# A graph attention layer in one pass: row windows kept in SBUF instead of a spill between stages, and one of two one-hot builds moved to ScalarE

## Chip, cores and metric

The kernel runs on one core of a Trainium2 chip. The metric is the device time of one execution in microseconds. The program is one launch; all work on the indices (sorting by source, positions, tile boundaries) is done on the chip.

## What is computed

The inputs are 3125 nodes with 256 features, and 50000 edges sorted by destination. The reference, cut to what matters:

```python
x = layernorm(x + relu(concat([x, segment_sum(w * x[dst], src)]) @ W + b))   # first layer
# then two graph attention layers, on the edges and one loop per node:
xl = (x @ Wl).reshape(n, 8, 32);  xr = (x @ Wr).reshape(n, 8, 32)
e = leaky_relu(xl[src] + xr[dst], 0.2)
score = einsum('ehc,hc->eh', e, att)
smax = segment_max(score, dst)
ex = exp(score - smax[dst]);  denom = segment_sum(ex, dst)
out = segment_sum(ex / denom[dst] * xl[src], dst) + b
x = x + gelu(out)
# at the end: x = layernorm(x1 + x), x1 being the result of the first layer
```

## The kernel before

The 50000 edges lie in blocks of 128 ("slots"): slot i has one edge on each of the 128 partitions, and all its edges have their destination in one tile of 128 nodes. A slot of edges at a tile boundary is present once for each of the tiles. There are 416 slots (`NI`), 104 groups of four (`G`, `NG`), 25 node tiles (`NT`) and 8 heads (`H`). All arithmetic is fp32.

The program is a row of stages with a barrier of all engines behind each. Within a stage every engine has its own loop over groups, and semaphores order them.

- Preparation (0 to 170 us): positions, tile tables, columns per slot, and `RST`, the reset table of the maxima.
- Scatter (170 to 826): for each group SyncE broadcasts the four slots' local destinations into `LBC` (two buffers, line 446), VectorE makes the transposed one-hot `OHT` of them (L458) and copies indices (L461, L462), PE expands node rows by it (L474), ScalarE weights them (L489), and GpSimd writes them to DRAM at their place by source (indirect transfers, L502).
- Sums by source (826 to 1074), the dense first layer and layer norm (to 1157).
- Then for each of two attention layers: a linear stage (1157 to 1232 in the first; VectorE's L829 to L848, 25 tiles), which also writes the table of rows (`tab_d`, 264 wide: 256 features and 8 linear score parts) to DRAM and keeps `TARGET`, the 272 wide part of the destinations, in SBUF;
- scoring (1232 to 1889): VectorE's one-hot (L927), PE's expansion of the destination's part (L913), GpSimd's indirect gather of the source's rows (L877) from indices that ScalarE copies (L980), the sum of both on VectorE (L934), Relu on ScalarE (L973), the weighting (L939) and reduction to scores (L942). SyncE writes every gathered group back to DRAM (`spill_d`, 544 KB for each group, L885);
- maxima (1889 to 1980): barred scores of all slots are transposed to rows, two scans forward and backward give the maximum of each destination over its run of edges (L1031 to L1048), with a trip to DRAM between for the carries between 16 chunks; then the shift and Exp for all slots (L1053, L1096);
- sums (1980 to 2294): 128 visits (104 groups and 24 boundaries). SyncE loads a spilled group (L1152), ScalarE appends its exponentials (L1174), VectorE and GpSimd weight two of its slots each (L1142), VectorE makes the one-hot `OH` of the destinations (L1198, L1203), PE multiplies (L1188), and VectorE adds the result to the tile's sums `ACC` (L1211);
- the close (2294 to 2350): the loop's own share, the division by the denominator, bias, Gelu and addition.

The second attention layer takes 2350 to 3527, a last layer norm ends at 3562. In the scoring stage VectorE's order is written by hand: one-hot of group q, sum of expansion and row of group q-1, score of group q-2. GpSimd fetches four groups ahead at most, into the four buffers of `GATH`, each of which is free when its spill has landed and Relu of its group is through.

## Time and profile before

| | us |
|---|---|
| median of 3 runs | 3580.03 |
| lowest, highest | 3555.76, 3587.68 |
| the profiled execution | 3563.68 |
| its span, first to last instruction | 3561.9 |
| mean granted TensorE clock, share of 2.4 GHz | 0.789 |
| PE busy | 1870.6 (53%) |
| VectorE (DVE) busy | 2152.1 (60%) |
| GpSimd (POOL) busy | 1762.4 (49%) |
| ScalarE (ACT) busy | 687.7 (19%) |
| moved by DMA | 559.52 MB |

In the rows further below, a line such as L934 is the kernel's line; "out<-in" are the program's names; x is a count; "idle before" is how long the engine had nothing to do before the instruction, and the arrow names what ended it, as far as the profile could tell. Indirect transfers on GpSimd show their issue, not their landing. Times of PE are modelled at their ends.

### The profile page before, as it was taken

What the parts mean: (1) busy time and instruction counts of PE and PEld (TensorE: products, weight loads), DVE (VectorE), ACT (ScalarE), POOL (GpSimd) and SP (SyncE); (2) the same over time, 40 slices, a digit from 0 to 9 for tenths busy, and PEclk for the clock granted to TensorE, in tenths of its full rate; (3) what the DMA queues carried; (4) which work ended last, traced back from release to release, by engine and by line L of the source; (5) the groups of instructions that cost most, each with busy time, mean ns of one, the idle gap of its engine ahead of it and who ended that gap; (6) DMA issues with size and microseconds to landing.
All of it is one profiled execution on the core that took longest, in us unless ns stands there. A gap on an engine that the chain in (4) does not pass through costs nothing. (4 is left out here: it accounts for less than half of the span.)

```text
span 3561.9 us, 40332 instructions
## 1 busy us (share of the span) xinstructions
PE 1870.6 (53%) x6284; PEld 1298.6 (36%) x6285; DVE 2152.1 (60%) x3331; ACT 687.7 (19%) x1987; POOL 1762.4 (49%) x1670
## 2 busy tenths in 40 slices
PE   0144444446996744544441688654454454248880
PEld 0133333335775323323321455422333333135560
DVE  6511111114664756666667799985666675779997
ACT  0022222220001322222221211132222221121111
POOL 0266666661002266666662455535666666325555
PEclk9976666668998866777675899977768777679995
DMA  1133333337991266666661577615666676237763
GB/s 54 23 108 101 101 100 103 100 101 205 266 261 40 76 193 189 206 190 206 187 205 37 183 225 231 200 36 164 193 199 213 195 214 200 68 124 228 231 218 110
DMA packets 271165, 559.52 MB, mean 157 GB/s; under 512 B 40988, under 2 KB 172352, under 8 KB 271134
## 3 DMA queue, kind: packets, MB, share of 16 engines
q1 hardware_dynamic: 210590, 394.18, 35.2%
q0 software_dynamic: 60544, 165.02, 16.4%
q14 instruction: 23, 0.19, 0.0%
q8 instruction: 8, 0.13, 0.0%
HBM read 377.24 MB, written 185.14 MB: 158 GB/s over the span
## 5 line engine op out<-in xcount | busy, mean ns | idle before, releaser
L877 POOL DMA_INDIRECT gath<-gather_table,GIDX x832 | 841.4, 1011 | 474.0 <-issue 257.6
L913 PE MATMUL p_expd<-node,OHT 128*128 x1664 | 615.5, 532 | 687.8 <-DVE OHT L927 487.3
L913 PEld LDWEIGHTS p_expd<-node,OHT 128*128 128x128 f32 x1664 | 406.0, 256 | 898.0 <-issue 803.3
L1188 PE MATMUL p_sums<-gath,OH 128*128 128x272 f32 x2048 | 536.9, 407 | 125.5 <-DVE OH L1203 101.2
L502 POOL DMA_INDIRECT rows_by_src<-gath,GIDX x416 | 411.7, 990 | 257.3 <-ACT gath L489 137.3
L1142 POOL TENSOR_TENSOR gath<-gath 128x512 f32<-128x512 f32 x256 | 323.7, 1266 | 435.1 <-ACT gath L1174 434.7
L934 DVE TENSOR_TENSOR work<-p_expd,gath 128x1056 f32<-128x1056 f32 x208 | 260.9, 1254 | 436.8 <-DMA chunk_carry<-by_head 182.4
L1188 PEld LDWEIGHTS p_sums<-gath,OH 128*128 128x128 f32 x2048 | 372.6, 191 | 289.4 <-issue 146.5
L474 PE MATMUL p_expd<-X,OHT 128*128 x832 | 285.8, 511 | 348.5 <-ACT gath L489 186.3
L474 PEld LDWEIGHTS p_expd<-X,OHT 128*128 128x128 f32 x832 | 208.8, 260 | 425.1 <-issue 385.5
L942 DVE TENSOR_REDUCE arena<-work 128x1056 f32 (+1 forms) x208 | 260.6, 1253 | 29.8
L939 DVE TENSOR_TENSOR work<-work,VEC 128x1024 f32<-128x1024 f32 x208 | 253.9, 1221 | 0.0
L489 ACT ACTIVATE gath<-p_expd,WGT 128x256 f32<-128x256 f32 x416 | 161.4, 481 | 467.9 <-remote 359.5
L580 PE MATMUL p_sums<-gath,OH 128*128 128x256 f32 x976 | 228.8, 388 | 42.5 <-DVE OH L553 41.8
L1203 DVE TENSOR_TENSOR OH<-iota_row,dst_local 128x512 f32<-128x512 f32 x256 | 250.9, 980 | 0.0
L458 DVE TENSOR_SCALAR OHT<-LBC,iota_p 128x512 f32<-128x512 bf16 x104 | 51.5, 496 | 325.2 <-remote 217.7
L971 ACT ACTIVATE arena<-p_expd 128x32 f32 (+1 forms) x208 | 41.2, 198 | 1008.2 <-DVE work L934 604.1
L973 ACT ACTIVATE work<-work 128x1024 f32<-128x1024 f32 x208 | 218.3, 1049 | 0.0
L580 PEld LDWEIGHTS p_sums<-gath,OH 128*128 128x128 f32 x976 | 181.6, 191 | 89.9 <-DVE OH L553 33.4
L1142 DVE TENSOR_TENSOR gath<-gath 128x512 f32<-128x512 f32 x256 | 193.7, 757 | 14.4 <-ACT gath L1174 13.1
L461 DVE CAST gath<-SRCI 128x4 f32 (+1 forms) x104 | 20.9, 201 | 226.8 <-DMA rows_by_src<-gath,GIDX 170.3
L1198 DVE TENSOR_TENSOR dst_local<-dst_visit,FIRST 128x4 f32<-128x4 f32 x256 | 121.6, 475 | 25.3 <-ACT dst_visit L1172 16.0
(189 smaller groups left out, 1781.5 us busy)
## 6 DMA issues: line engine op xcount, KB each, us to landing
gath<-gathered SPq DMA_DIRECT2D x256, 544.0 KB
gathered<-gath SPq DMA_DIRECT2D x208, 544.0 KB
gath<-rows_by_src SPq DMA_DIRECT2D x122, 514.0 KB
LBC<-local_rows SPq DMA_DIRECT2D x312, 128.0 KB
gath<-gather_table,GIDX POOLq DMA_INDIRECT x832
rows_by_src<-gath,GIDX POOLq DMA_INDIRECT x416
gather_table<-arena SPq DMA_DIRECT2D x50, 132.0 KB, 1.7
arena<-gather_table SPq DMA_DIRECT2D x10, 640.0 KB
```

Source lines behind the costliest of these rows:

```text
L474: ins = pe.matmul(expd[s % 2][:, g // 2, (g % 2) * D:(g % 2 + 1) * D], OHT[:, s % 2, g * P:(g + 1) * P], Xv[:, bass.ds(j, 1), :], start=Tr ...
L502: pool.indirect_dma_start(sup_d[:, :], bass.IndirectOffsetOnAxis(GIDX[:, s, g:g + 1], 0), U[:, s, g, :], None, bounds_check=EP - 1, oob_is ...
L580: ins = pe.matmul(sums[s][:, 0:D], OH[:, s % 2, g, :], U[:, s, g, 0:D], start=(g == 0), stop=(g == G - 1))
L877: pool.indirect_dma_start(GATH[:, s, g, 0:XW], None, tab_d[:, :], bass.IndirectOffsetOnAxis(GIDX[:, s, g:g + 1], 0)).then_inc(gathered[s], 16)
L913: ins = pe.matmul(expd[s % 2][:, g, 0:RW], OHT[:, s % 2, g * P:(g + 1) * P], TARGET[:, bass.ds(j, 1), :], start=True, stop=True)
L934: dve.tensor_tensor(Zv[:, s4 % 2], expd[s4 % 2][:, :, 0:XW], GATH[:, s4, :, 0:XW], ALU.add).then_inc(z_ready, 1)
L939: dve.tensor_tensor(TR, TR, VEC[:, 2, :].rearrange("p (h c) -> p h c", h=H).unsqueeze(1).broadcast_to([P, G, H, C]), ALU.mult).then_inc(we ...
L942: dve.tensor_reduce(SC[:, bass.ds(G * H * q, G * H)], T[:, s2, :].rearrange("p (g c) -> p g c", c=C + 1), AX, ALU.add).then_inc(scored, 1)
L973: act.activation(Tv[:, s % 2, :, :, 0:C], Zv[:, s % 2, :, 0:D].rearrange("p g (h c) -> p g h c", h=H), ACT.Relu).then_inc(relu_ready, 1)
L1142: return eng.tensor_tensor(V, V, GATH[:, s, g0:g1, D:D + H].unsqueeze(3).broadcast_to([P, g1 - g0, H, C]), ALU.mult)
L1188: ins = pe.matmul(sums[s][:, 0:RW], OH[:, s % 2, g, :], GATH[:, s, g, :], start=(g == 0), stop=(g == G - 1))
L1203: dve.tensor_tensor(OH[:, s % 2], iota_row[:, :].unsqueeze(1).broadcast_to([P, G, P]), LS[:, s % 2, :].unsqueeze(2).broadcast_to([P, G, P] ...
```

## The change

The three stages scoring, maxima and sums of an attention layer become one, in which everything is unrolled.

- Slots come in pairs of one tile, so 440 rather than 416 slots, and 110 groups of four. Four groups are a window of 16 slots, of which there are 28. One slot's 8 heads by 16 slots are 128 columns.
- Gathered rows stay in `ROWS`, a ring of 12 groups in SBUF; there is no spill. The indices are read from `SRCI` itself. GpSimd gathers group q behind its share of the weighting of group q-10.
- A group's score is made as before. When a window's scores are there, VectorE bars them (`bar`), PE transposes them, and VectorE scans forward and backward over 128 columns (`ends`), works out the carries between slots on one partition (`carry`), scans again with them (`maximum`), and shifts (`shift`); ScalarE makes the exponentials and a factor `GROW`, by which the sums of a tile that reaches over a window's boundary are scaled (`grow`). The carries go through PE, not DRAM.
- Sums are taken eight steps (`LAG`) behind the expansion, two tiles per group and so two additions into `ACC` (`add_sums`).
- The one-hot of the sums is made by ScalarE: |column - destination| for each slot (`own`), then Relu(1 - that) for four (`own_end`). The transposed one-hot of the expansion stays on VectorE (`hot`).
- The score of a node's own loop is no longer expanded per slot but kept per node (`OWN`), and joins at the close, where the edges' sums are scaled by Exp of the difference of maxima. The linear stage forms less for it.
- `LBC` has four buffers, also in the scatter stage, which is unrolled too and loses the copy at L462.
- Preparation fetches one more column (next destination), and the tables of resets are per window.

```diff
+PAIRS = (NB + 2 * NT - 1) // 2
+NI = -(-2 * PAIRS // G) * G
+K = P // H
+WG = K // G
+NW = -(-NI // K)
+RING = 3 * WG
+LAG = 2 * WG
...
-                                dve.tensor_tensor(LIN, LR[:, s, :, 0:D], VEC[:, 1, :].unsqueeze(1).broadcast_to([P, 2, D]),
-                                                  ALU.mult).then_inc(lin_ready, 1)
+                                dve.tensor_tensor(LIN, LR[:, s, 0, 0:D], VEC[:, 1, :], ALU.mult).then_inc(lin_ready, 1)
...
+                    @block.sync
+                    def _(sp):
+                        for q in range(NG):
+                            if q >= 4:
+                                sp.wait_ge(hot_t, q - 3)
+                            sp.dma_start(LBC[:, q % 4, :], locals_of(q)).then_inc(loc_in[q % 4], 16)
 
                     @block.gpsimd
                     def _(pool):
+                        def gather(q):
+                            if q >= RING:
+                                pool.wait_ge(summed, q - RING + 1)
+                            pool.nop(nofuse=True)
+                            for g in range(G):
+                                i = G * q + g
+                                pool.indirect_dma_start(ROWS[:, i % (RING * G), 0:XW], None, tab_d[:, :],
+                                                        bass.IndirectOffsetOnAxis(SRCI[:, i:i + 1], 0)).then_inc(gathered[q % RING], 16)
+
+                        for q in range(NG + RING - 2):
+                            a = q - RING + 2
+                            if a >= 0:
+                                pool.wait_ge(exps, a // WG + 1)
+                                weigh(pool, a, 0, 2).then_inc(by_pool, 1)
+                            if q < NG:
+                                gather(q)
...
+                        expand(0)
+                        for t in range(STEPS):
+                            if t + 1 < NG:
+                                expand(t + 1)
+                            u = t // WG - 1
+                            if 0 <= u < NW and t % WG == 0:
...
+                                pe.wait_ge(barred, u + 1)
+                                pe.transpose(BY_ROW, BARRED[:, :, :].rearrange("p h k -> p (h k)"), ident[:, :]).then_inc(by_row, 1)
...
+                            a = t - LAG
+                            if 0 <= a < NG:
+                                pe.wait_ge(hots, a + 1)
+                                pe.wait_ge(by_pool, a + 1)
+                                pe.wait_ge(by_dve, a + 1)
+                                pe.wait_ge(added, 2 * a)
+                                for g in range(G):
+                                    ins = pe.matmul(sums[g // 2][:, 0:RW], OH[:, a % 2, g, :], slots(a, g, g + 1)[:, 0, :], start=(g % 2 == 0), stop=(g % 2 == 1))
+                                ins.then_inc(summed, 1)
...
+                        def ends(u):
+                            dve.wait_ge(by_row, u + 1)
+                            if u:
+                                dve.wait_ge(final, u)
+                            dve.tensor_scalar(HOT[:, :], iota_row[0:1, :], NLOC[0:1, K * u:K * u + 1], 0.0, ALU.add, ALU.is_equal)
+                            link(dve.tensor_tensor_scan(FWD[:, :], RST[:, u, 0:P], BY_ROW, -BIG, ALU.add, ALU.max))
+                            dve.tensor_tensor_scan(BWD[:, ::-1], RST[:, u, 1:P + 1][:, ::-1], FWD[:, ::-1], -BIG, ALU.add, ALU.max).then_inc(ends_ready, 1)
...
+                        def add_sums(a, tiles):
+                            dve.wait_ge(summed, a + 1)
+                            for k in range(2):
+                                j = tiles[2 * (a % WG) + k]
+                                dve.tensor_tensor(ACC[:, bass.ds(j, 1), :], ACC[:, bass.ds(j, 1), :], sums[k][:, 0:RW].unsqueeze(1), ALU.add).then_inc(added, 1)
+                                dve.wait_ge(added, 2 * a + k + 1)
...
+                        for t in range(STEPS):
+                            if due(t, 2):
+                                shift(t // WG - 2)
+                            if t < NG:
+                                add(t)
+                            if t + 2 < NG:
+                                hot(t + 2)
+                            u = t // WG - 1
+                            if 0 <= u < NW and t % WG:
+                                (ends, carry, maximum)[t % WG - 1](u)
+                            if 0 < t <= NG:
+                                score(t - 1)
+                            if due(t, 1):
+                                bar(u)
+                            a = t - LAG
+                            if 1 <= a <= NG:
+                                add_sums(a - 1, tiles)
+                            if a >= 0 and a % WG == 0 and a < NG:
+                                tiles = tiles_of(dve, 2 * a, 2 * groups(a // WG))
+                                if a:
+                                    grow(a // WG, tiles[0])
+                            if 0 <= a < NG:
+                                dve.wait_ge(exps, a // WG + 1)
+                                weigh(dve, a, 2, G).then_inc(by_dve, 1)
...
+                        def own(a):
+                            if a >= 2:
+                                act.wait_ge(summed, a - 1)
+                            for g in range(G):
+                                i = G * a + g
+                                ins = act.activation(OH[:, a % 2, g, :], iota_row[:, :], ACT.Abs, bias=NLOC[:, i:i + 1])
+                            ins.then_inc(near, 1)
+
+                        def own_end(a, n):
+                            act.wait_ge(near, n)
+                            act.activation(OH[:, a % 2], OH[:, a % 2], ACT.Relu, bias=ones[:, 0:1], scale=-1.0).then_inc(hots, 1)
```

## Rows read from the trace of the kernel before

**Rows 1.** Windows by stage: stretch, length, busy us of PE, PEld, DVE, ACT, POOL (instructions), clock, DMA share, GB/s

```profile
170.00:826.00 656.00, 285.78 (x832) 208.83 (x832) 75.98 (x312) 162.68 (x417) 414.71 (x417) 0.69 0.33 99
...
1157.00:1232.00 75.00, 56.49 (x150) 24.54 (x150) 61.69 (x177) 30.11 (x75) 11.65 (x25) 0.91 0.19 64
1232.00:1889.00 657.00, 303.70 (x832) 199.59 (x832) 415.20 (x416) 141.99 (x417) 427.01 (x416) 0.72 0.64 195
1889.00:1980.00 91.00, 11.16 (x52) 10.12 (x52) 57.47 (x24) 14.95 (x18) 17.66 (x3) 0.52 0.03 6
1980.00:2294.00 314.00, 267.82 (x1024) 186.24 (x1024) 302.64 (x510) 58.97 (x255) 160.73 (x128) 0.99 0.72 225
```

**Rows 2.** Timeline of DVE in the scoring stage: start us, us, engine, line, operation

```profile
1504.08 0.48 DVE L927 TENSOR_SCALAR OHT<-LBC,iota_p 128x512 f32<-128x512 bf16 x1
1504.47 1.25 DVE L934 TENSOR_TENSOR work<-p_expd,gath 128x1056 f32<-128x1056 f32 x1
1505.64 1.22 DVE L939 TENSOR_TENSOR work<-work,VEC 128x1024 f32<-128x1024 f32 x1
1507.01 1.25 DVE L942 TENSOR_REDUCE arena<-work 128x1056 f32 x1
1508.18 0.48 DVE L927 TENSOR_SCALAR OHT<-LBC,iota_p 128x512 f32<-128x512 bf16 x1
```

**Rows 3.** Groups of instructions: count, busy us and mean ns of one, idle before, releaser

```profile
L1142 POOL TENSOR_TENSOR gath<-gath 128x512 f32<-128x512 f32 x256 | 323.7, 1266 | 435.1 <-ACT gath L1174 434.7
...
L973 ACT ACTIVATE work<-work 128x1024 f32<-128x1024 f32 x208 | 218.3, 1049 | 0.0
...
L1211 DVE TENSOR_TENSOR node<-node,p_sums 128x272 f32 x256 | 108.8, 425 | 3.0 <-PE p_sums L1188 2.2 <-DVE node L1211 0.8
...
L975 ACT ACTIVATE work<-work 128x32 f32<-128x32 f32 x208 | 51.7, 248 | 0.0
...
L1092 ACT ACTIVATE arena<-p_f 128x512 f32<-128x512 f32 (+1 forms) x28 | 15.1, 568 | 137.3 <-PE p_f L1082 114.5 <-PE p_f L1073 22.7
...
L1096 ACT ACT_TABLE_LOAD x2 | 2.6, 1283 | 0.0
```

**Rows 4.** Timelines of DVE and POOL in the sums stage

```profile
2127.64 0.69 DVE L1142 TENSOR_TENSOR gath<-gath 128x512 f32<-128x512 f32 x1
2128.25 1.54 DVE L1203 TENSOR_TENSOR OH<-iota_row,dst_local 128x512 f32<-128x512 f32 x1
...
2127.69 1.55 POOL L1142 TENSOR_TENSOR gath<-gath 128x512 f32<-128x512 f32 x1 [1.80 <-ACT gath L1174]
```

**Rows 5.** Groups of instructions: small operations and scans of DVE

```profile
L1047 DVE TENSOR_TENSOR_SCAN gath<-arena,carries 128x3328 f32<-128x3328 f32 x2 | 14.3, 7151 | 22.9 <-DMA carries<-chunk_carry 22.9
...
L840 DVE TENSOR_TENSOR arena<-arena 128x8 f32<-128x8 f32 x50 | 7.9, 157 | 0.0
...
L1040 DVE TENSOR_TENSOR_SCAN by_head<-by_head 8x16 f32<-8x16 f32 x2 | 0.4, 178 | 9.6 <-DMA by_head<-chunk_summary 9.6
```

**Rows 6.** A stall in scoring (POOL, DVE); its waits, 1240 to 1880: us, times, longest

```profile
1514.31 0.96 POOL L877 DMA_INDIRECT gath<-gather_table,GIDX  x1 [0.30 <-issue]
...
1515.59 1.26 DVE L934 TENSOR_TENSOR work<-p_expd,gath 128x1056 f32<-128x1056 f32 x1 [6.94 <-DMA FIRST<-step_tables]
...
DVE work L934 <- DMA FIRST<-step_tables: 166.3, 23, 11.4
```

**Rows 7.** Timelines of POOL and ACT in the scatter stage

```profile
454.89 0.98 POOL L502 DMA_INDIRECT rows_by_src<-gath,GIDX  x1 [0.30 <-issue]
461.33 0.98 POOL L502 DMA_INDIRECT rows_by_src<-gath,GIDX  x1 [5.46 <-ACT gath L489]
...
458.92 1.21 ACT L489 ACTIVATE gath<-p_expd,WGT 128x256 f32<-128x256 f32 x3 [11.06 <-remote]
```

**Rows 8.** Timeline of PE: one group's expansion, then one group's sums

```profile
1509.53 3.18 PE L913 MATMUL p_expd<-node,OHT 128*128 x8 [2.24 <-issue]
...
2289.53 2.10 PE L1188 MATMUL p_sums<-gath,OH 128*128 128x272 f32 x8
```

More of the change, by code:

```diff
@@ L861, in build @@
[L861 to L867 removed]
+                expd = [ps(f"expd{k}", [P, 2, 512]) for k in range(2)]
+                sums = [ps(f"sums{k}", [P, 512]) for k in range(2)]
+                cols = ps("cols", [P, 512])
+                rows = ps("rows", [P, 512])
+                BY_ROW, FINAL = cols[:, 0:P], cols[:, P:2 * P]
@@ L929, in add, with hot @@
-                        def add(q, s4, turn4, first):
-                            dve.wait_ge(gathered[s4], 64 * (turn4 + 1))
-                            dve.wait_ge(exp_ready, q + 1)
-                            if not first:
+                        dve.memset(SC[:, :, :], 0.0)
+                        dve.memset(BARRED[:, :, :], -BIG)
+                        link(dve.memset(line[:, :], -BIG))
+                        dve.memset(CR[:, :], 0.0).then_inc(set_up, 1)
+                        def hot(q):
+                            dve.wait_ge(loc_in[q % 4], 16 * (q // 4 + 1))
+                            if q >= 2:
+                                dve.wait_ge(expanded, q - 1)
+                            dve.tensor_scalar(OHT[:, q % 2, :], LBC[:, q % 4, :], iota_p[:, 0:1], None, ALU.is_equal).then_inc(hot_t, 1)
```

874 lines of the change are left out of this document (387 added, 487 removed).

## Prediction

> **What bounds the kernel now.** I read first the windows by stage [rows 1], to see which engine is full in each stage that the change touches. The first graph layer's middle is three stages: the expansion and scoring (657 us), the maxima (91) and the sums (314), 1062 us in all; I take the second layer for the same. In the sums VectorE is full (302.6 of 314). In the scoring nobody is: VectorE works 415 of 657 us, GpSimd 427, and the DMA engines move 195 GB/s, to which the spill of the gathered rows belongs. In the maxima all engines together do little.
>
> Then VectorE's timeline in a stretch of the scoring without stalls [rows 2]: from one start of L927 to the next are 4.10 us for a group of four slots. That is less than its four instructions one by one (4.20), since the end of one overlaps the start of the next; behind L939, where the next waits for a semaphore of its own engine, it does not (1.37 us from start to start for 1.22 of work, 0.15 for the link). A group needs four row transfers of GpSimd, each 0.96 us behind a gap of 0.30, 5.06 us [rows 6]. So GpSimd's transfers, 104 x 5.06 = 526 us, are the floor of the scoring, and some 130 us are stalls. What they look like is in [rows 6]: the sum at L934 starts at 1515.59 after 6.94 us of idleness, when GpSimd has just finished its last queued transfer (1514.31 + 0.96). Such waits are 166 us in 23 pieces in this stage. The scatter stage ahead (170 to 826) has the same shape with no spill at all: 104 groups in 656 us, 6.3 us each, though GpSimd issues them in 5.15 (0.98 and a gap of 0.30 each); again and again it falls quiet, as for 5.46 us behind the transfer at 454.89 [rows 7].
>
> **The change, part by part.** (1) *The new single pass.* 110 groups of four slots in windows of four groups; a group is summed eight steps after it is expanded. VectorE's work for a step in the middle: the expansion's sum, now 1024 wide (1.14 from start to start), the one-hot (0.39), weighting with its link (1.37) and the reduction (1.17): 4.07 us [rows 2]. Then two additions into the node sums for one before, 128x272 at 0.42 [rows 3], each with a link of 0.15: 1.14. Then half of the weighting of the rows, 0.60 from start to start [rows 4]. The one-hot for the sums, 0.68 here, has gone to ScalarE. Together 5.81 us.
>
> Once per window come the maxima. Small operations cost 0.16 (8 wide) [rows 5] to 0.42 (272 wide) [rows 3], so 0.28 at 128; a scan has a fixed 0.14 and 2.1 ns a column (178 ns for 16 columns, 7.15 us for 3328), so 0.42 for 128 [rows 5]. Barring and shifting: three of 128, 0.8. `ends`: one small, two scans and a link, 1.1. `carry`: two scans, three copies or sums of 128, four of 8 and five links, 3.1, less four overlaps of 0.08, 2.8. `maximum`: one small, two scans, two links, 1.3. `grow`: one of 256, one of 8, a link, 0.7. The register loads, a guess by the link's size, 0.4. Sum 7.1, or 1.78 a step. So 7.6 us a step before anyone disturbs anyone.
>
> Of contention the sums stage has the nearest row, since there too GpSimd weights two slots per group beside VectorE: a weighting of 1.55 us on GpSimd stands over a VectorE instruction of 1.54 that elsewhere takes 0.68 [rows 4]. Over the stage VectorE is busy 302.6/128 = 2.36 us a visit, where its four instructions undisturbed need 0.68 + 0.68 + 0.42 + 0.16 = 1.94 [rows 1, 3, 4, 5]: 0.42 lost per GpSimd weighting. Bounds are 0 and 0.86 (every one collides in full); I take 0.42, for the same pair of operations is in the row. A step is 8.0 us. [...]
>
> (2) *Who else could set the step.* GpSimd: 5.06 for the transfers plus 1.27 for the weighting [rows 3] and gaps, 6.6 us: under 8.0, with some 5 us over per window. PE: eight passes for the expansion and eight for the sums take 2.1 us each at full clock (the second of [rows 8]), and eleven small ones per window, by the same 0.26 a pass, 0.75 a step: 5 us. ScalarE: Relu 1.05 and its tail 0.25, the one-hot as four of 128 columns (0.3 each, between nothing and the 0.57 for 512) and one of 512 (0.57): 3.1, with the window's six small ones 3.5 [rows 3]. All three lie under VectorE's step, and their results are asked for a step later: the sums of group a-1 begin when its weighting ends, need 2.1 us, and VectorE comes to add them 4 us into the next step. So the one-hot on ScalarE costs nothing, as long as VectorE's 8.0 us cover it. Exp, Relu, Abs and Copy alternate in a window. One table load takes 1.28 us and stands once per layer for Exp [rows 3]; four loads per window would be 1.3 us a step on ScalarE, still covered. By "ScalarE: Activation LUTs", section "Table sets: the hidden batching unit", in the Trainium skill all of these lie in one set and none is needed; the trace agrees, with no load at the Relu that follows another layer's Gelu.
>
> (3) *The pass as a whole.* The first eight steps have no sums and go at GpSimd's pace: 8 x 5.1 and 3 of landing, with one stall like that of [rows 6] 52 us. 102 full steps: 816. The tail of eight, in which weighting, PE's 2.1, addition and little else follow each other, 3.6 us each: 29. The stage's start, 3. Sum 900, against 1062: -162 a layer, -324 for two. No spill is written or read back; as no stage waits for DMA bandwidth in the new order, that is in the figure already.
>
> (4) *The scatter stage.* 110 groups rather than 104, four buffers for the local rows rather than two, one copy less. At its old 6.3 us a group, 693: +37. If the buffers take the stalls away, 110 x 5.15 + 10 = 577: -79. But in such a spell ScalarE too starts only at 458.92, 3 us after GpSimd's last transfer, though it does not wait for those buffers [rows 7]; so I keep +37.
>
> (5) *Smaller ones.* Preparation: four more transfers (5), two reductions of 3584 columns (8), some ten small chained operations (3), strided loads (4): +20. The linear stage (75 us, VectorE 61.7 of it): per tile one multiplication and one reduction 256 wide rather than 512, and a small sum less, 0.7 us, 17 in 25 tiles; PE is busy 56 us there, so I take -12 a layer. The memset of the sums goes to its end on GpSimd, which has been done by then. The closing stage: six more operations of 200 columns and two Exps with a wait, +3 a layer; the large multiplication by the denominators is only replaced. The first dense stage loses a memset: -1.
>
> Sum: -324 + 37 + 20 - 24 + 6 - 1 = -286. From the span of 3562: 3276; the run is 2 longer than its span, and the median of the runs 16 above the profiled one: 3294, said as 3295.
>
> **The rivals.** *R1, the stalls come along (slower).* VectorE is full in the new pass, so a late arrival ahead of its sum of expansion and row is lost time. The place is the wait of `add` for rows and expansion. For it: these waits stand in both stages with GpSimd transfers [rows 6, 7], and in the new pass each transfer group leads its use by only two steps at the start of a window. Against: GpSimd is at it 5.06 of 8.0 us (63%), not 5.15 of 6.3 (82%), with a weighting in between and a spell of quiet per window, and the spill is gone. Price as now, 166 us x 110/104 = 176 a layer: 3295 + 352 = 3647. It decides from 142 us a layer on, 1.3 us a step. *R2, every GpSimd weighting collides in full*: 0.44 x 204 = +90: 3385. *R3, PE's clock stays at 1.2 GHz, the lower of its two levels.* Then eight passes take up to twice 2.1 us (3.18 in the first of [rows 8], where the clock was low for a part), the step 4.2 + 4.2 + 1.5 = 9.9, and PE is the bound: +388, 3683. Against it: with PE at work 5 of 8 us, more than in the scoring stage (46% and clock 0.72), it should hold. *R4, better all round*: no collisions (-86) and the scatter stage without stalls (-116): 3093. That the change does not do what it says is no case here: the stages are gone from the program.
>
> **How the numbers follow.** The forecast 0.5 (own range 3230 to 3350), R1 0.18, R2 0.15, R3 0.05, R4 0.12. The range, 3110 to 3580, leaves out most of R1 and R3 and the end of R4. About 1% is what a measurement of this kernel can tell from no change (its three runs span 0.9%). Faster: forecast, R2 and R4, 0.77, and 0.01 of R1, whose price may be half. Within 1%: 0.05, from R1 and R3 near the threshold. Slower: the rest of them, 0.17.
>
> **What would show it.** In the profile after: one stage per layer of some 890 us with VectorE over 90% busy; start to start of the sum of expansion and row 7.5 to 8.4 us in the middle; the added idleness ahead of that sum under 50 us a layer (R1: over 150); GpSimd's weighting near 1.3 us and VectorE's own at 0.7 to 0.9 (R2: over 1.3); the clock over 0.9 in the pass (R3: under 0.7); the scatter stage near 690 us. I am wrong if a serial exchange between VectorE and PE inside a window, which I let overlap, shows as idleness of VectorE, or if the 25 small operations per window cost far more than 7.1 us.

## The result, and the profile after

The changed kernel takes 3318.7 us in the median (3312 to 3327) beside 3580.8 for the kernel before: a ratio of 0.928 (95% interval 0.923 to 0.933). Forecast were 3295 us and a range of 3110 to 3580; the time lies 24 us above the forecast.

For what follows one thing has to be known: the kernel before itself runs at two levels, 3332 to 3338 us in some sittings (runs made together on one chip) and 3546 to 3581 in others, so only runs of one sitting, or stages that do not depend on it, are compared below.

Table 1: the length of each stage, from the first VectorE instruction of one to that of the next, in the two profiled executions (before 3561.9 us, after 3316.4 us).

| stage | before | after | difference | forecast |
|---|---|---|---|---|
| preparation | 171.2 | 192.1 | +21 | +20 |
| scatter | 656.4 | 669.7 | +13 | +37 |
| sums by source | 254.8 | 255.2 | 0 | 0 |
| first dense stage | 83.0 | 82.1 | -1 | -1 |
| linear, both layers | 71.2 + 71.4 | 55.4 + 56.1 | -31 | -24 |
| middle of layer 1 | 1058.8 | 928.7 | -130 | -162 |
| middle of layer 2 | 1049.4 | 929.2 | -120 | -162 |
| close, both layers, and end | 145.8 | 148.0 | +2 | +6 |
| sum | | | -245.5 | -286 |

The forecast's sum was 41 us too good. It came out only 24 us too low, since 16 us, the distance of the median from the profiled run of before, were added and did not come again. Of the 74 us that the two middles gained less than forecast, 58 are the new passes (929 us each instead of 900) and 16 the base: I had put the old middles at 1062 us each, and they measured 1059 and 1049.

First the windows of the profile after: the scatter stage, the new pass of layer 1, and a stretch of its middle; then the same pass in three parts. The columns are those of [rows 1].

```profile
192.00:862.00 670.00, 306.83 (x880) 221.69 (x880) 68.37 (x221) 172.06 (x441) 434.99 (x441) 0.68 0.35 99
1254.00:2183.00 929.00, 601.54 (x2124) 449.90 (x2124) 813.32 (x1332) 354.56 (x939) 589.96 (x550) 0.79 0.32 80
1350.00:2050.00 700.00, 467.18 (x1696) 354.05 (x1695) 651.66 (x1057) 280.67 (x748) 472.05 (x442) 0.81 0.33 85
...
1254.00:1324.00 70.00, 32.23 (x91) 22.33 (x92) 37.41 (x55) 12.18 (x24) 41.40 (x41) 0.65 0.38 104
1324.00:2124.00 800.00, 532.81 (x1935) 403.07 (x1933) 745.17 (x1205) 322.86 (x861) 542.45 (x504) 0.81 0.34 84
2124.00:2183.00 59.00, 36.51 (x100) 24.49 (x100) 30.74 (x74) 19.52 (x55) 6.11 (x6) 0.68 0.00 1
```

In the middle VectorE is busy 651.66 of 700 us, 93%: it is what sets the step, as forecast. The start, 70 us with VectorE half idle, and the end, 59 us, are not full. The granted clock is 0.81 in the middle, not over 0.9.

These are VectorE's groups in the same middle, 1350 to 2050 us (columns as in [rows 3]):

```profile
L1033 DVE TENSOR_TENSOR work<-p_expd,gath 128x1024 f32<-128x1024 f32 x88 | 107.1, 1217 | 3.3 <-PE p_expd L971 3.2
L1099 DVE TENSOR_TENSOR node<-node,p_sums 128x272 f32 x176 | 76.1, 432 | 12.6
L1106 DVE TENSOR_TENSOR node<-node,grow 128x256 f32 x22 | 32.3, 1469 | 17.4 <-issue 14.2 <-DVE node L1099 3.2
L1073 DVE TENSOR_TENSOR line<-line 1x8 f32<-1x8 f32 x22 | 24.6, 1120 | 0.8
L1071 DVE COPY line<-line 1x8 f32<-1x8 f32 x22 | 9.8, 447 | 0.8
```

Ahead of L1033, the sum of expansion and row, VectorE waits 3.3 us in 88 steps. That is the place of rival R1, and next to nothing is lost there. But an instruction of 8 columns takes 1.12 us in the mean (its neighbour of the same size 0.15), and the rescaling of a node tile, L1106, takes 1.47. What they wait for is seen when VectorE's and GpSimd's timelines of one window are laid side by side. VectorE:

```profile
1900.26 1.90 DVE L1106 TENSOR_TENSOR node<-node,grow 128x256 f32 x1 [0.79 <-DVE node L1099]
...
1907.82 1.01 DVE L1099 TENSOR_TENSOR node<-node,p_sums 128x272 f32 x2
...
1912.68 0.15 DVE L1072 TENSOR_TENSOR line<-line 1x8 f32<-1x8 f32 x1
1912.86 1.65 DVE L1073 TENSOR_TENSOR line<-line 1x8 f32<-1x8 f32 x1
1914.54 0.15 DVE L1074 TENSOR_TENSOR line<-line 1x8 f32<-1x8 f32 x1
1914.63 1.21 DVE L1039 TENSOR_TENSOR work<-work,VEC 128x1024 f32<-128x1024 f32 x1
```

and GpSimd:

```profile
1900.81 1.06 POOL L933 TENSOR_TENSOR gath<-gath 128x512 f32<-128x512 f32 x1
...
1907.45 1.06 POOL L933 TENSOR_TENSOR gath<-gath 128x512 f32<-128x512 f32 x1
...
1912.46 0.94 POOL L952 DMA_INDIRECT gath<-gather_table,SRCI  x1 [0.30 <-issue]
1913.41 1.06 POOL L933 TENSOR_TENSOR gath<-gath 128x512 f32<-128x512 f32 x1
1914.63 2.07 POOL L952 DMA_INDIRECT gath<-gather_table,SRCI  x1 [0.16 <-issue]
```

The 8-column sum at 1912.86 ends at 1914.51, when GpSimd's weighting has ended (1913.41 + 1.06 = 1914.47); L1106 ends at 1902.16, just behind the weighting that ends at 1901.87. Both start some 0.55 us before the recorded start of the weighting whose end they share (1912.86 against 1913.41, 1900.26 against 1900.81); why so early, these rows do not say. The additions at 1907.82, with an input in PSUM, keep their 1.01 us for two although a weighting runs beside them. And it goes the other way too: the transfer that GpSimd issues at 1914.63, the moment VectorE's L1039 begins, takes 2.07 us instead of 0.94.

### The profile page after: what moved, and what is told of

Same layout as the page of the kernel before. It is cut to its first block and busy times, and to the rows that moved or that the text cites. A ratio compares the mean times of both kernels' runs of the same rounds, so it can differ in the third digit from the quotient of the medians.

```text
span 3316.4 us, 30379 instructions
## 1 busy us (share of the span) xinstructions
PE 1910.8 (58%) x6768; PEld 1410.9 (43%) x6768; DVE 2217.8 (67%) x3985; ACT 980.3 (30%) x2514; POOL 1774.5 (54%) x1707
## 5 line engine op out<-in xcount | busy, mean ns | idle before, releaser
L952 POOL DMA_INDIRECT gath<-gather_table,SRCI x880 | 945.1, 1074 | 261.6 <-issue 232.4
L1009 PE MATMUL p_sums<-gath,OH 128*128 128x272 f32 x1760 | 658.4, 536 | 486.2 <-DVE gath L933 480.1
L525 POOL DMA_INDIRECT rows_by_src<-gath,node x440 | 430.1, 977 | 270.6 <-ACT gath L514 140.7
L971 PE MATMUL p_expd<-node,OHT 128*128 x1760 | 481.4, 423 | 39.4 <-DVE OHT L1026 24.4
L933 POOL TENSOR_TENSOR gath<-gath 128x512 f32<-128x512 f32 x220 | 234.0, 1066 | 407.2 <-ACT gath L1172 404.6
L514 ACT ACTIVATE gath<-p_expd,node 128x256 f32<-128x256 f32 x440 | 170.8, 479 | 478.9 <-remote 358.3
L1033 DVE TENSOR_TENSOR work<-p_expd,gath 128x1024 f32<-128x1024 f32 x220 | 267.8, 1217 | 50.1 <-remote 23.5
L1153 ACT ACTIVATE OH<-iota_row,NLOC 128x128 f32<-128x128 f32 x880 | 278.7, 387 | 60.4 <-PE p_sums L1009 56.1
L1043 DVE TENSOR_REDUCE scores<-work 128x32 f32<-128x1056 f32 x220 | 275.7, 1253 | 7.6
L1039 DVE TENSOR_TENSOR work<-work,VEC 128x1024 f32<-128x1024 f32 x220 | 265.6, 1207 | 0.0
L1099 DVE TENSOR_TENSOR node<-node,p_sums 128x272 f32 x440 | 190.3, 432 | 79.4 <-PE p_sums L1009 47.2
L933 DVE TENSOR_TENSOR gath<-gath 128x512 f32<-128x512 f32 x220 | 153.7, 699 | 8.1 <-issue 0.6
```

Source lines behind the costliest of these rows:

```text
L525: pool.indirect_dma_start(sup_d[:, :], bass.IndirectOffsetOnAxis(POSI[:, i:i + 1], 0), U[:, q % 4, g, :], None, bounds_check=EP - 1, oob_i ...
L933: return eng.tensor_tensor(R, R, V[:, :, D:XW].unsqueeze(3).broadcast_to([P, g1 - g0, H, C]), ALU.mult)
L952: pool.indirect_dma_start(ROWS[:, i % (RING * G), 0:XW], None, tab_d[:, :], bass.IndirectOffsetOnAxis(SRCI[:, i:i + 1], 0)).then_inc(gathe ...
L971: ins = pe.matmul(expd[q % 2][:, g // 2, (g % 2) * D:(g % 2 + 1) * D], OHT[:, q % 2, g * P:(g + 1) * P], TARGET[:, bass.ds(tiles[g // 2], ...
L1009: ins = pe.matmul(sums[g // 2][:, 0:RW], OH[:, a % 2, g, :], slots(a, g, g + 1)[:, 0, :], start=(g % 2 == 0), stop=(g % 2 == 1))
L1033: dve.tensor_tensor(Zv[:, q % 2].rearrange("p k (g n) -> p k g n", g=2), expd[q % 2][:, :, :].rearrange("p k (g n) -> p k g n", g=2), slot ...
```

## The experiments

All kernels are the changed one with the edit shown, unless said otherwise. Where a step is given, it is the time between the starts of the sum of expansion and row (L1033, in some variants L1029, L1027 or L1023), taken over 88 steps in the middle of layer 1's pass. This figure is the same in every sitting: 7.96, 7.96 and 7.95 us for the three kernels in which the middle of the pass is the changed kernel's (`after`, `ctl_after`, `early`).

**First sitting: the kernel before 3331.7 us.** Four kernels, the first on the pass, the others on the stalls of the scatter stage.

*h_dve*, the one-hot for the sums back on VectorE:

```diff
+ dve.scalar_tensor_tensor(OH[:, a % 2], iota_row..., -1.0, NLOC[:, G*a:G*a+G]..., ALU.mult, ALU.is_equal).then_inc(hots, 1)
  weigh(dve, a, 2, G).then_inc(by_dve, 1)
...
- own(a)
- own_end(a, a + 1)
```

> The changed kernel with the one-hot for the sums made by VectorE again (one instruction of 128x512 just ahead of its weighting), ScalarE's five instructions for it taken out. Theory (VectorE's own work sets the step of the single pass): each of the 102 full steps grows by the 0.68 us that this instruction took in the kernel before, so the pass by some 70 us a layer and the kernel from 3319 to about 3460; with collisions (it reads two inputs in SBUF beside GpSimd's weighting) up to 3530. Rival (the step is set by the exchange of VectorE with ScalarE and PE, or by GpSimd's transfers): VectorE has slack, and the time moves by less than 30 us.

Measured: 3301.2 us, 0.990 of the kernel before (0.988 to 0.993). The changed kernel itself takes 3194.4 in the next sitting, which is of the same kind, and its three variants below take 3192 to 3196 in this one. So the one-hot on ScalarE is worth 107 us of the 143 that the change brings in such a sitting; the rest of the change takes off 1% there. The step goes from 7.96 to 8.45: 0.49 us, less than 0.68. From the one-hot's start to the next instruction's are 0.61 us; 0.05 comes back because VectorE now loses 0.65 us a step to GpSimd's weighting and not 0.70 (the sum is shown under *w_dve*), and some 0.04 because the wait ahead of L1033 is gone. The theory holds, VectorE has next to no slack.

*s_pace*, a paced queue in the scatter stage:

```diff
  pool.wait_ge(u_ready, q + 1)
+ if q >= 3:
+     pool.wait_ge(scattered[(q - 3) % 4], 64 * ((q - 3) // 4 + 1))
```

> The changed kernel with one more wait in the scatter stage: GpSimd issues the transfers of a group only when those of the group three before have landed, so that the transfers under way at once are fewer. Theory P (the stalls of this stage come from a backlog of transfers, behind which everything else that travels by DMA queues up): with fewer under way the stalls go, the stage falls from 670 us to between 580 and 620, the kernel to 3230 to 3270. Rival (the backlog only sits in the queue and has nothing to do with the stalls): the stage stays at 670 or grows by the wait, to 700, the kernel at 3320 to 3350.

*s_tick*, a small computing instruction between the groups:

```diff
  pool.wait_ge(u_ready, q + 1)
+ pool.memset(TICK[:, q:q + 1], 0.0)
```

> The changed kernel with one small computing instruction of GpSimd (a memset of one column) ahead of each group of the scatter stage. Theory G (the stalls arise while GpSimd issues transfers back to back with nothing in between, which the single pass with its weighting never does once it runs full): the stalls of 8 to 12 us every seven groups go, the stage falls from 670 us to about 110 x 5.3 + 10 = 590, the kernel to 3240. Rival (the stalls are of the transfers, whatever GpSimd does in between): the stage stays at 660 to 680 us and the kernel at 3315 to 3330.

*s_two*, two local-row buffers in the scatter stage, as before:

```diff
- if q >= 4: sp.wait_ge(hot_ready, q - 3)
- sp.dma_start(LBC[:, q % 4, :], locals_of(q)).then_inc(loc_in[q % 4], 16)
+ if q >= 2: sp.wait_ge(hot_ready, q - 1)
+ sp.dma_start(LBC[:, q % 2, :], locals_of(q)).then_inc(loc_in[q % 2], 16)
```

> The changed kernel with two instead of four buffers for the local rows in the scatter stage, as before: that part of the change undone. In the prediction this edit was taken at nothing. Theory: the stalls do not hang on these buffers, the stage stays at 660 to 690 us and the kernel at 3310 to 3345. Rival (the buffers have taken some of the stalls away, and so the stage came out at 670 and not at the 693 forecast): the stage at 693 or more, the kernel at 3342 or more.

Measured: 3196.1, 3194.2 and 3192.3 us. Three different edits, one result, and a kernel before 250 us faster than the one first read: read against the 3319 us, each edit would have looked like the cure. None of them is. *h_dve* leaves the scatter stage as it is, and there too the stage takes 581 us in this sitting, as in the other three (581, 581 and 581). All three expectations had been written against the wrong base. Whether one of the edits would help where the stalls are, no run shows.

**Second sitting: the kernel before 3337.8 us.**

*ctl_after* is the changed kernel unaltered.

> The changed kernel itself, unaltered, as the control. Three variants of its scatter stage (a paced queue, a small instruction in between, two local-row buffers) all came out at 3192 to 3196 us beside a kernel before of 3332, though the times first shown for the two were 3319 and 3581. Theory S (the stalls with GpSimd's transfers are a matter of the chip the kernel runs on, not of the three edits): on a chip where the kernel before takes some 3330 us this one takes 3190 to 3200, a ratio of 0.958; on one where it takes some 3580 it takes 3310 to 3330, a ratio of 0.928. Rival (each of the three edits breaks the stalls): beside a kernel before of 3330 it takes 3300 or more.

Measured: 3194.4 us (3192 to 3195), ratio 0.958 (0.954 to 0.961). That is the figure of theory S, and the rival is out: the three edits of the first sitting are worth nothing there. That the level belongs to the chip is not shown. The first sitting and the third and fourth ran on a chip of the same number, 6, and the kernel before took 3332 us in the one and 3546 and 3551 in the others.

*ctl_before* is the kernel before, unaltered.

> The kernel before itself, unaltered, for its trace on this chip. Theory S: if its time here is some 3330 us, the 250 us less than in the trace first read lie in the stages with GpSimd's transfers: the scatter stage at 5.1 to 5.3 us a group, 540 to 560 us instead of 656, the two scoring stages at 550 to 590 us each instead of 657, and its waits of some 7 us that go as 'remote' gone. Rival (the whole chip is faster): the sums stages (314 us) and the source sums are shorter by 5% or more too.

Measured: 3333.9 us, span 3332.1. The windows of the scatter stage, layer 1's scoring and layer 1's sums in this sitting:

```profile
171.00:731.00 560.00, 305.35 (x832) 213.10 (x832) 82.08 (x312) 164.52 (x417) 415.69 (x417) 0.73 0.44 117
1139.00:1725.00 586.00, 337.93 (x832) 220.32 (x832) 419.88 (x416) 154.66 (x412) 450.67 (x415) 0.70 0.76 218
1812.00:2130.00 318.00, 268.50 (x1024) 186.56 (x1024) 304.54 (x511) 58.90 (x255) 159.30 (x128) 0.98 0.72 224
```

Against [rows 1]: scatter 560 instead of 656, scoring 586 instead of 655, the sums stage the same. VectorE's and GpSimd's busy times are no shorter (GpSimd's 416 and 451 us beside 415 and 427); only waits are gone. In this sitting the page also has a time from issue to landing for the scatter's transfers:

```profile
gath<-gather_table,GIDX POOLq DMA_INDIRECT x832, 3.7
rows_by_src<-gath,GIDX POOLq DMA_INDIRECT x416, 3.5
```

and the longest waits of the scatter stage are regular ones, many and short, with nothing that ends as "remote":

```profile
DVE gath L461 <- DMA rows_by_src<-gath,GIDX: 425.9, 100, 6.8
PEld p_expd L474 <- issue: 276.9, 95, 6.3
ACT gath L489 <- DVE GIDX L462: 276.3, 74, 5.5
```

The scatter stage of the changed kernel with stalls (3318 us) looks otherwise:

```profile
ACT gath L514 <- remote: 358.3, 41, 16.7
DVE OHT L488 <- remote: 209.1, 33, 12.1
```

So the stalls of [rows 6, 7] cost the kernel before 96 us in the scatter stage and 68 and 65 in the two scoring stages: 230 us, all of the difference between its two levels. In the changed kernel they cost 90 in the scatter stage and 12 and 18 in the two passes; over the whole span it is 124 us (3316.4 against 3192.8). What makes them come and go between sittings, no run here shows. They also set what the change is worth: by the profiled spans 245 us with the stalls and 139 without (by the medians 262 and 143).

*w_dve*, GpSimd weights nothing:

```diff
- weigh(pool, a, 0, 2).then_inc(by_pool, 1)
- pe.wait_ge(by_pool, a + 1)
- weigh(dve, a, 2, G).then_inc(by_dve, 1)
+ weigh(dve, a, 0, G).then_inc(by_dve, 1)
```

> The changed kernel with all four slots of a group weighted by VectorE and none by GpSimd. Theory C (GpSimd's weighting costs VectorE some 0.4 us per step by contention, as the prediction had it): VectorE's instruction goes from 0.70 to 1.2 us, the collisions go, a step grows by 0.1 to 0.3 us, the pass by 10 to 30 us a layer, the kernel by 20 to 60 us over the control. Rival N (no contention to speak of): plus 0.6 x 102 = 61 us a layer, 120 in all. Rival F (contention costs more than the half weighting saves): no more than the control, or less.

Measured: 3163.0 us (3162 to 3164), 31 us less than the control; step 7.72. It is rival F. Here are its groups in the middle:

```profile
L933 DVE TENSOR_TENSOR gath<-gath 128x1024 f32<-128x1024 f32 x85 | 104.3, 1227 | 3.0
L1022 DVE TENSOR_SCALAR OHT<-LBC,iota_p 128x512 f32<-128x512 bf16 x83 | 39.9, 481 | 0.0
L1102 DVE TENSOR_TENSOR node<-node,grow 128x256 f32 x21 | 8.9, 425 | 16.6 <-DVE node L1095 16.6
```

The rescaling is down from 1469 to 425 ns, with nothing changed about it but that GpSimd no longer computes. The other victims fall too. That gives the price of contention in the changed kernel, per window of four steps: (1469 - 425) ns for L1106, (1120 - 159) for L1073, (447 - 193) for L1071, four times (561 - 481) for the one-hot, 220 on two more of `carry`: 2.8 us, 0.70 us a step. The half weighting that GpSimd takes over is worth 1.15 - 0.61 = 0.54 from start to start. GpSimd's help costs more than it brings: 0.16 us a step by these rows, 0.24 by the step, of which 0.04 is the wait ahead of L1033 that is gone too.

*hg_act*, the one-hot for the expansion and the rescaling of a node tile go to ScalarE too:

```diff
+ act.activation(OHT[:, q % 2, :], LBC[:, q % 4, :], ACT.Abs, bias=minus_p[:, 0:1]).then_inc(far, 1)
+ act.activation(OHT[:, q % 2, :], OHT[:, q % 2, :], ACT.Relu, bias=ones[:, 0:1], scale=-1.0).then_inc(hot_t, 1)
+ for h in range(H):
+     R = ACC[:, bass.ds(tile, 1), h * C:(h + 1) * C]
+     ins = act.activation(R, R, ACT.Copy, scale=GROW[:, h:h + 1])
- dve.tensor_scalar(OHT[:, q % 2, :], LBC[:, q % 4, :], iota_p[:, 0:1], None, ALU.is_equal).then_inc(hot_t, 1)
- dve.tensor_tensor(R, R, GROW[:, :].unsqueeze(2).broadcast_to([P, H, C]), ALU.mult)
```

> The changed kernel with two more pieces of VectorE's work on ScalarE: the one-hot for the expansion too (Abs and Relu over 128x512), and the rescaling of a node tile at each window's start (eight instructions of 128x32 with a factor per partition). Theory (VectorE sets the step): VectorE loses 0.45 us a group and 1.4 us a window, so 110 x 0.45 + 27 x 1.4 = 87 us a layer, 170 in all: the ratio to the control about 0.947, start to start of the expansion's sum 7.1 instead of 7.9 us. GpSimd, with 5.0 + 1.1 us and gaps a step, is then near. Rival (with ScalarE at 5 us a step and more exchange, the chain through ScalarE and PE sets the step): less than 60 us of gain, or a loss, with VectorE idle at the sum of expansion and row or at the additions of the sums.

Measured: 3044.6 us (3043 to 3046), 0.913 of the kernel before (0.910 to 0.916) and 150 us less than the control; step 7.21. The theory, with a gain 20 us smaller than it gave; ScalarE's added work is hidden.

**Third sitting: the kernel before 3546.1 us.**

*h_act* has only the first of these two moves.

> The changed kernel with only the one-hot for the expansion moved to ScalarE too (the rescaling of the node tile stays on VectorE): the first half of the run with both moves, to split its gain of 150 us. Theory (VectorE's own work adds up to the step): start to start of this instruction is 0.39 to 0.48 us, 110 groups, two layers: 85 to 105 us less than the control's 3194, so 3090 to 3110, a step of 7.5 us, and the other 45 to 65 us of the double move belong to the rescaling. Rival (the instruction filled time in which VectorE would have waited for GpSimd's lock anyway): the wait moves to the next instruction with two inputs in SBUF, and the gain is under 60 us.

Measured: 3182.7 us, a ratio of 0.898 (0.896 to 0.901). The times in the expectation were for the other kind of sitting, so the step has to decide: 7.26 us. It gains 0.70, not 0.39 to 0.48, and the rescaling brings only 0.05 more. The groups of its middle say why:

```profile
L1033 DVE TENSOR_TENSOR work<-work,VEC 128x1024 f32<-128x1024 f32 x97 | 124.1, 1280 | 0.0
L933 DVE TENSOR_TENSOR gath<-gath 128x512 f32<-128x512 f32 x96 | 84.9, 885 | 3.3
L1060 DVE TENSOR_TENSOR_SCAN line<-line 1x136 f32<-1x136 f32 x24 | 16.0, 665 | 0.8
L1100 DVE TENSOR_TENSOR node<-node,grow 128x256 f32 x24 | 10.2, 425 | 19.3 <-DVE node L1093 18.2 <-issue 1.1
```

With one instruction fewer in the step GpSimd's weighting meets others. The rescaling is back at 425 ns and the 8-column sum at 0.16 us, while the weighting (885 for 690), the multiplication (1280 for 1205) and one scan (665 for 429) now take longer: 0.35 us a step instead of 0.70. So about half the gain is VectorE's instruction taken away, and the other half is contention that fell away with it. The theory was right in its kind, not in its split. The rival is out.

*hgw* has both moves, and VectorE weights all four slots.

> The kernel with both moves to ScalarE, and in addition all four slots weighted by VectorE, none by GpSimd. In the control the same edit gained 31 us. Theory (what GpSimd's weighting costs VectorE depends on which instructions it happens to meet, and can be summed from the excess of each row over its undisturbed time): with both moves that excess is 0.27 + 0.06 on the weighting and the multiplication and 0.3 us a window on a scan, 0.43 us a step in all instead of 0.8, so giving GpSimd's half back to VectorE (0.61) costs 0.18 a step: 3045 + 37 = 3080. Rival (the cost is a constant of each weighting): the gain of 31 us comes again, 3014.

Measured: 3203.3 us, a ratio of 0.904 (0.901 to 0.906). The expected 3080 and 3014 us were for a sitting without stalls, and hg_act did not run in this one, so again the step has to decide: 7.27, against 7.21 for hg_act. The same edit that gained 0.24 us a step in the changed kernel costs 0.06 here. That decides against the rival (a constant price per weighting); the sum from the rows, +0.18, has the sign right and is 0.12 too high; 0.07 of that is the half weighting, taken as 0.61 and worth 0.54.

*early* weights a group before the sums of the group ahead are added:

```diff
+ weigh(dve, a, 2, G).then_inc(by_dve, 1)
  add_sums(a - 1, tiles)
  ...
- weigh(dve, a, 2, G).then_inc(by_dve, 1)
```

> The changed kernel with VectorE weighting group a before, not behind, the addition of the sums of group a-1. Theory (the last eight groups of a pass go at 6 to 7 us each, not at the 3.6 of the prediction, because weighting, PE's sums at its lower clock, addition and the next weighting follow each other in a ring): PE's sums of a group can start right behind the additions, the ring loses the 0.7 us of the weighting, 8 groups, two layers: 10 to 15 us less, 3180 to 3185, and the middle of the pass stays at 7.96 us a step. Rival (in the middle the later additions hold up PE's next sums): the step grows and the kernel with it, 3200 or more.

Measured: 3271.5 us, a ratio of 0.923 (0.921 to 0.926). The changed kernel had 0.928 (0.923 to 0.933) in another sitting of this kind; the intervals overlap, and the times in the expectation were for a sitting without stalls. So the trace has to decide. This is PE in the last steps of the changed kernel's pass:

```profile
2164.56 3.06 PE L1009 MATMUL p_sums<-gath,OH 128*128 128x272 f32 x8 [2.04 <-DVE gath L933]
2170.80 3.97 PE L1009 MATMUL p_sums<-gath,OH 128*128 128x272 f32 x8 [3.18 <-DVE gath L933]
2176.80 3.97 PE L1009 MATMUL p_sums<-gath,OH 128*128 128x272 f32 x8 [2.03 <-DVE gath L933]
```

and VectorE beside it:

```profile
2169.86 0.69 DVE L933 TENSOR_TENSOR gath<-gath 128x512 f32<-128x512 f32 x1
2174.81 1.02 DVE L1099 TENSOR_TENSOR node<-node,p_sums 128x272 f32 x2 [4.26 <-PE p_sums L1009]
2175.86 0.69 DVE L933 TENSOR_TENSOR gath<-gath 128x512 f32<-128x512 f32 x1
2180.91 1.02 DVE L1099 TENSOR_TENSOR node<-node,p_sums 128x272 f32 x2 [4.37 <-PE p_sums L1009]
```

Each waits for the other in turn: weighting, PE's sums, addition, weighting, a ring of 6.0 us a group. In `early` the stretch from the last L1033 to the end of the pass is 45 us, in the changed kernel 59 and in the control 62, while the middle keeps its 7.95 us: the rival, a longer step, is out. The end gave back more than the 0.7 us a group expected, 1.8 to 2.1. Its two halves in `early` (columns as in [rows 1]), with PE's sums in them, show what the rest is:

```profile
2108.00:2130.00 22.00, 16.42 (x43) 10.53 (x41) 15.84 (x35) 9.35 (x27) 3.88 (x4) 0.52 0.00 0
2130.00:2153.00 23.00, 13.36 (x56) 9.27 (x55) 14.40 (x40) 9.91 (x29) 3.25 (x3) 1.00 0.00 1
...
2125.25 3.97 PE L1009 MATMUL p_sums<-gath,OH 128*128 128x272 f32 x8 [1.09 <-DVE node L1099]
...
2134.42 2.07 PE L1009 MATMUL p_sums<-gath,OH 128*128 128x272 f32 x8 [1.22 <-DVE node L1099]
2138.13 2.07 PE L1009 MATMUL p_sums<-gath,OH 128*128 128x272 f32 x8 [1.20 <-DVE node L1099]
```

From 2130 on the granted clock is 1.00, the eight passes take 2.07 us instead of 3.97, and the groups follow each other at 3.3 to 3.9 us. In the changed kernel the clock of the whole end is 0.68 and in the control 0.64, and at most one of their ten groups has 2.07 us. So the larger part of what `early` brought is PE's clock at the end of the pass, the smaller the order. Whether the order is what raised the clock, one profile does not show.

**Fourth sitting: the kernel before 3550.5 us.** *hge* puts hg_act and early together.

> All that has gained put together: both one-hots and the rescaling of the node tile on ScalarE, and VectorE's weighting ahead of the addition of the sums. Theory (the gains are independent: 0.75 us a step for the moves, some 17 us a pass at its end for the order): beside a kernel before of 3330 to 3340 it takes 3045 - 34 = 3010, a ratio of 0.90; beside one of 3550 to 3580 some 3140, a ratio of 0.885. Start to start 7.2 us in the middle, and 45 us or less from the last sum of expansion and row to the end of the pass, instead of 62. Rival (with the step at 7.2 us the later additions hold up PE's next sums, and VectorE waits for them): the ratio stays where the double move without the new order had it, 0.913 in the first case.

Measured: 3161.0 us (3156 to 3168), a ratio of 0.889 (0.887 to 0.892), the best of all in a sitting of this kind: 0.928 for the change alone, 0.898 for h_act. The theory had 0.885 and some 3140 us. The end of the pass is 48 us, but the step 7.29, not 7.21. VectorE does not wait longer for PE's sums, as the rival had it (13.2 us of idleness ahead of 179 additions in the middle, 12.6 ahead of 172 in hg_act). GpSimd's weighting has found another victim, the last 8 columns of the rescaling:

```profile
L1101 DVE TENSOR_TENSOR node<-node,grow 128x8 f32 x23 | 38.3, 1663 | 18.7 <-DVE node L1095 15.4 <-issue 3.3
```

It takes 0.17 us in hg_act and 1.66 here: 0.37 us a step more. Some 0.2 of that comes back at other instructions (the weighting 824 ns instead of 913, a scan 428 instead of 764), which leaves about the 0.08 by which the step is longer, and a little over.

## Why the prediction came out as it did

**The step of 8.0 us: right, by terms that were off and cancel.** It measured 7.96. VectorE's own instructions for a step take 5.62 us in the timeline instead of 5.81 (the additions 1.04 for two instead of 1.14, multiplication and reduction 2.41 instead of 2.54, the one-hot 0.42), the window's small ones about 1.64 a step instead of 1.78. In the 1.78 the part for `ends` was summed as 1.1 us a window, where its own terms give 1.27; with it the forecast of the step would have been 0.04 longer. Contention, taken as 0.42 from [rows 4], is 0.70. It was within the bounds of 0 and 0.86, but the row gave its size and not its victims. In the sums stage the victim was a large instruction; here VectorE's own weighting stays at 0.69, and what pays is whichever instruction the weighting happens to meet, down to one of 8 columns. The Trainium skill's page "SBUF — State Buffer", section "Who interferes with whom", says that the shared ports are an exclusive lock, in which the later one waits for the whole instruction of the other; the trace agrees (1914.51 against 1914.47). The size of the waiting instruction therefore says nothing of the price. That the step came out at 8.0 all the same is luck: contention 0.28 too low against the other terms 0.33 too high.

**ScalarE's one-hot at nothing: right.** h_dve undid it and lost 107 us, and it is the larger part of what the change is worth without stalls. Its four small instructions take 0.387 us and the large one 0.707, not 0.3 and 0.57, and still vanish under the step: ScalarE is busy 280.67 of 700 us. Here is the row of the small one:

```profile
L1153 ACT ACTIVATE OH<-iota_row,NLOC 128x128 f32<-128x128 f32 x880 | 278.7, 387 | 60.4 <-PE p_sums L1009 56.1
```

The rows by which I went had no factor or offset per partition. One with a factor stood in the same trace, L489 of the scatter stage with 481 ns for 256 columns, and it lies between the two. The Trainium skill's page "ScalarE: Activation LUTs", section "What ACT_TABLE_LOAD costs", gives 280 ns and 0.833 ns a column with an offset per partition. The estimate from it is 387 ns for 128 columns and 707 for 512; both rows agree. Of table loads the trace after has one a layer for Exp, as before, and none inside a window.

**The pass: 900 forecast, 929 measured.** By its parts: start and first eight groups 69 instead of 55; the 102 steps from there 809 instead of 816; the tail 51 instead of 29.

- The tail is the larger miss. I had let weighting, PE and addition follow each other at 3.6 us, with PE's eight passes at 2.1, their time at the higher clock. Most of them take 3 to 4 us there at a granted clock of 0.68, as the first of [rows 8] could have told, and the ring takes 6.0 us a group. With the clock at 1.00, in the second half of `early`'s end, the groups do follow at 3.3 to 3.9 us. The term that was off is above all PE's time for its eight passes, up to 3.97 us instead of 2.1, at the lower clock: 1.9 of the 2.4 us between 3.6 and 6.0. The prediction named a serial exchange between VectorE and PE as a way to be wrong; it came in the tail only.
- The start: one stall. The gap between the sixth and the seventh L1033 is 18.4 us, and in the control it is 5.4 and the whole stretch 52 us. The forecast of 52, and 3 for the stage's start, had one stall of some 8 us in it; without any the start takes that long already. The long gap adds 13 and the two ahead of it 4, and it is 69.

**The stalls do not come along: right, and it is 106 of the 245 us.** R1 had asked whether the 166 us of waits of [rows 6] go over into the new pass. In the middle of the pass VectorE waits 3.3 us at that place, and 50 us in both layers together (the sign for R1 was over 150 in one). The stalls stand where GpSimd issues transfer after transfer and the others have no lead, in the scatter stage and in the first steps of the pass. In the middle GpSimd rests some 6 us once a window (5.57 ahead of the weighting at 1926.41) and has two groups or more of lead. The counter-argument in the prediction (63% of GpSimd's time instead of 82%, with pauses) was of the right kind. hgw, in which GpSimd computes nothing at all in the pass, ran in a sitting with stalls (its scatter stage takes 658 us) and has none in its middle either, with a wait of 0.4 us in 90 steps. So a computing instruction in between is not needed. That leaves the pauses and the lead, and no run separates them. That the gain itself depends on the sitting, 245 us or 139, I had not seen.

**The scatter stage: +37 forecast, +13 measured.** 110 groups at 6.1 us instead of 6.3. Why the groups came shorter is open. The prediction asked whether the four buffers help; s_two says no (581 us, as in h_dve, where the stage is unaltered) where there are no stalls. Where there are, it was not tried. The rival figure of 577 us for a stage without stalls was exact (580 in the control), but it is not the buffers that bring it.

**The linear stages** gained 16 us each instead of 12, preparation and dense stage came as worked out, the close within 4 us.

**R3**: the clock is 0.81 in the middle, under the 0.9 I had named as a sign and far over the 0.7 of the rival. PE waits for the end of VectorE's weighting, 480 us in both passes, and is at work 67% of the middle; in the old sums stage it was at work 85% at a clock of 0.99 [rows 1]. In the middle VectorE, 93% busy, hides it; in the tail it shows.

```profile
L1009 PE MATMUL p_sums<-gath,OH 128*128 128x272 f32 x1760 | 658.4, 536 | 486.2 <-DVE gath L933 480.1
```

**R2**, every weighting colliding in full (0.86 a step), was nearer than I held it to be: 0.70. It was hidden by the other terms being 0.33 too high. The sign that I had named for it, VectorE's own weighting over 1.3 us, would have missed it: that instruction stayed at 0.69, and others paid.

## What to carry to other kernels

Where two engines share a lock, price the contention by the length of the instruction that holds it, up to all of it, not by that of the one that waits (0.70 us here for a weighting of 1.06), and then ask whether the work handed over saves more than it holds; here GpSimd's half of the weighting did not, until the other edits had moved it beside other instructions (0.42 us lost a step in hg_act for 0.54 gained). The time of an added or removed instruction on the engine that sets the step is only half of its effect: it also shifts what runs beside what (h_act gained 0.70 us a step for an instruction of 0.42, and in hge a reordering cost 0.08). And run the unaltered kernel beside the variants in the same sitting: three edits would each have passed for a cure worth 125 us.

## What the runs showed of the hardware

- Transfers that GpSimd issues row by row have two levels of behaviour for one and the same program: a stage of 110 groups takes 580 to 584 us or 658 to 670, the latter with waits of up to 12.1 us at VectorE and 16.7 at ScalarE. The difference of 230 us in the kernel before lies wholly in the stages with these transfers. What sets the level is open; runs on a chip of the same number showed both.
- VectorE's instructions with both inputs in SBUF also hold up GpSimd's issue of a transfer: 2.07 us instead of 0.94 where it begins with L1039. In the middle of the pass 61 of the 65 transfers that begin while L1039 or L933 runs take over 1.05 us; of the 128 that begin during L1033, L1043 or L1099, which have at most one input in SBUF, none does.
- Copies and comparisons with a single tensor input in SBUF wait for GpSimd's weighting as well: the one-hot 561 ns instead of 481, a copy of 8 columns 447 instead of 193, and 1718 in `early`. The section "Who interferes with whom" of the Trainium skill's page "SBUF — State Buffer" has this for `copy`, `cast` and `tensor_scalar` instructions that run in a two-port mode; that they wait, the rows show, in which mode they ran no run here shows.
